# Moving VectorE's pieces, a split W2 load, SyncE stores and a cyclic field order in a three-layer CIN tower

## The reference

```python
def _cin_layer(X0, Xi, W, b):            # X0 (512, 39, 16), Xi (512, 39 or 128, 16)
    Wr = W.reshape(H, F0_, Fi)           # H = 128
    return jnp.einsum('hjk,bjd,bkd->bhd', Wr, X0, Xi) + b[None, :, None]

Xi = X0
for W, b in Ws:                          # three layers
    Xi = _cin_layer(X0, Xi, W, b)
    res.append(Xi.sum(axis=2))
z = jnp.concatenate(res, axis=1)         # (512, 384)
h = jnp.concatenate([z, dense_ctx], axis=1)
h = jnp.maximum(h @ W_top1 + b_top1, 0.0)
h = jnp.maximum(h @ W_top2 + b_top2, 0.0)
y = h @ W_top3
```

## Time and profile before

| | us |
|---|---|
| median of three runs | 679.05 |
| the profiled execution, whole | 682.02 |
| its span, first to last instruction | 680.2 |
| TensorE busy | 631.0 |
| VectorE busy | 582.5 |
| ScalarE busy | 549.5 |
| GpSimd busy | 431.7 |

### The profile page before, as it was taken

How to read it: one execution, slowest core, us unless ns; L and a number is a source line. 1 busy time by engine, 2 the same in 40 slices (tenths; PEclk the granted TensorE clock), 3 DMA queues, 4 the chain that set the end, 5 groups by cost and what they waited for, 6 DMA issues and landing times.

```text
span 680.2 us, 14168 instructions
## 1 busy us (share of the span) xinstructions
PE 631.0 (93%) x2563; PEld 473.1 (70%) x2563; DVE 582.5 (86%) x1229; ACT 549.5 (81%) x1735; POOL 431.7 (63%) x409
## 2 busy tenths in 40 slices
PE   0489799999999999999999999999999999999998
PEld 0157577777777777777777777777777777767583
DVE  0558769999989898999999999989898989999880
ACT  2057498989898989889898989898989889898682
POOL 6758396868868686868595968868685636220000
PEclk9989989999999999999999999999999999999999
DMA  6533712223140404040312223140404031000200
GB/s 219 140 78 81 229 47 74 68 51 89 27 115 9 131 3 124 16 119 21 94 47 63 78 53 88 25 116 8 132 2 128 9 106 32 12 17 0 63 0 1
DMA packets 42545, 46.14 MB, mean 68 GB/s; under 512 B 20705, under 2 KB 25409, under 8 KB 42378
## 3 DMA queue, kind: packets, MB, share of 16 engines
q1 hardware_dynamic: 26146, 42.28, 21.1%
q0 software_dynamic: 5120, 1.32, 2.4%
q10 hardware_dynamic: 11239, 2.05, 1.7%
HBM read 44.30 MB, written 1.31 MB: 67 GB/s over the span
## 4 chain that ended last, share of the span: by engine, by line
PE 54%; issue 20%; DVE 16%; DVEq 5%; DMA 2%; SPq 1%; POOL 1%; ACT 0%; ACTq 0%; POOLq 0%
DVE chain L614 8%; PE ya L493 7%; PE ya L494 6%; PE ya L495 6%; PE acc L469 6%; PE yd L493 5%; PE yd L495 5%; PE yd L494 5%; PE misc L476 3%; DVE z L641 2%; DVEq L146 2%; DVE prods L614 2%; DMA x0a<-x_rows 2%; DVEq L614 1%; DVE chain L612 1%
## 5 line engine op out<-in xcount | busy, mean ns | idle before, releaser
L740 ACT ACTIVATE prods<-ya,x0t 128x128 f32<-128x128 f32 x1472 | 451.6, 509 | 64.5 <-PE ya L495 59.9
L614 DVE SCALAR_TENSOR_TENSOR chain<-yd,x0t,chain 128x128 f32<-128x128 f32 x768 | 218.5, 344 | 16.3 <-PE yd L495 10.7
L301 POOL TENSOR_TENSOR prod<-tiles,x0a 120x512 f32<-120x512 f32 x105 | 136.6, 1302 | 83.5 <-DMA tiles<-x_rows 66.4
L493 PE MATMUL ya<-w1h,x1h 128*128 128x512 f32 (+1 forms) x384 | 173.8, 452 | 7.9 <-ACT prods L740 5.8
L373 POOL DMA_INDIRECT emb<-in_tables,rows x160 | 157.1, 982 | 36.3 <-issue 27.1
L494 PE MATMUL ya<-w1l,x1h 128*128 128x512 f32 (+1 forms) x384 | 147.9, 385 | 0.0
L495 PE MATMUL ya<-w1h,x1l 128*128 128x512 f32 (+1 forms) x384 | 147.5, 384 | 0.0
L629 DVE TENSOR_REDUCE x2t<-prods 128x128 f32<-128x1792 f32 x64 | 129.2, 2019 | 8.7 <-ACT prods L740 6.3
L493 PE MATMUL yd<-w1h,x1h 128*128 128x512 f32 x256 | 104.6, 409 | 11.1 <-DVE prods L614 6.7
L629 DVE TENSOR_REDUCE prods<-prods 128x128 f32<-128x1536 f32 x64 | 111.8, 1747 | 0.0
L408 POOL TENSOR_TENSOR prod0l<-prod,prod0h 120x512 fp32r<-120x512 f32 x70 | 91.1, 1301 | 27.1 <-ACT prod0h L749 26.9
(11 more groups left out here) (96 smaller groups left out, 602.8 us busy)
## 6 DMA issues: line engine op xcount, KB each, us to landing
tiles<-x_rows SPq DMA_DIRECT2D x236, 78.0 KB
x0a<-x_rows SPq DMA_DIRECT2D x45, 80.0 KB
emb<-in_tables,rows POOLq DMA_INDIRECT x160
w<-in_w SPq DMA_DIRECT2D x3, 832.0 KB
w<-in_w SPq DMA_DIRECT2D x1, 2496.0 KB, 12.8
tiles<-x_rows SPq DMA_DIRECT2D x32, 42.0 KB
x<-x_rows SPq DMA_DIRECT2D x16, 78.0 KB
x<-x_rows SPq DMA_DIRECT2D x16, 77.8 KB
```

Source lines behind the costliest of these rows:

```text
L301: engine.tensor_tensor(prod0[:, i % L0_PRODS, :], tiles[:, slot, :], x0a[:, :], ALU.mult).then_inc(prod0_ready, 1)
L493: pe.matmul(out, x1h[:, c % 2, xs], w1h[:, cols], start=True, stop=False)
L614: dve.scalar_tensor_tensor(out, product, x, run if step else b1[:, :], ALU.mult, ALU.add).then_inc(yd_used, 1)
L740: mm = act.activation(prods[:, :, slot_of(q) + i], ya[(NA * g + k) % YA][:, i * H:(i + 1) * H], ACT.Copy, scale=turned(c)[:, g * F1 + j:g ...
```

## The change

1. **VectorE's pieces.** `sum_dims` moves from group 1 to group 2, behind D block 3. `split_x1` moves from group 3 behind D block 6 to group 3 behind D block 3.
2. **W2 in 13 pieces** of three fields (192 KB), one after the loads of each chunk from 2 to 14.
3. **Stores on SyncE.** The store of a chunk's rows is issued by SyncE instead of ScalarE, as four DMAs instead of two: rows 40 to 59 of the scratch repeat rows 0 to 19.
4. **A cycle of 40.** Shifts are taken modulo 40 (39 fields and the padding row, whose weight is zero), as `tile + 7u`. With the repeated rows no shift wraps, so tile i and tile i+1 are the same rows one further, and one DMA of 40 partitions by 4 KB loads two of them. A chunk takes 12 tile DMAs instead of 28. In chunk 0 the last three tiles get places of their own in `gram`.
5. **The start.** Three matmuls (`WARM`) on TensorE after chunk 0's rows are stored; `turn_x0(0)` after layer-0 step 5 instead of 2; for chunk 0 ScalarE makes the rounded half straight from `acc0`, and VectorE makes the low half in two parts, so that TensorE's group 0 waits for the first 128 columns only; the low part of `w0` is made after that.

```diff
+SHIFTS = 7
+XR = FP + FP // 2
-TURN_0 = 2
+TURN_0 = 5
+WARM = 3
+W2_PARTS = 13
+BATCHES = ((0, 2), (2, 4), (4, 6), (6, 7))
+SUM_DIMS, SPLIT_X1 = (2, 0), (3, 0)
...
-def segments(i):
...
+        def load_tiles(engine, x, b):
+
+            first, end = BATCHES[b]
+            wait_done(engine, prod0_ready, max(uses_before(i, L0_TILES, x) for i in range(first, end)) if x else 0)
...
+            for u in range(3):
+                row = x * XR + SHIFTS * u + first
+                rows_on = bass.AP(scratch.tensor, row * COLS, [[COLS, R0], [1, (end - first) * COLS]])
+                engine.dma_start(to[u * R0:(u + 1) * R0, :, :].rearrange("p i n -> p (i n)"), rows_on).then_inc(tile_in[b], 16)
...
             def load_layer0(x, nxt):
 
-                sp.wait_ge(scratch_in, 2 * 16 * (x + 1))
+                sp.wait_ge(scratch_in, 4 * 16 * (x + 1))
                 wait_done(sp, prod0_ready, T0 * x)
                 load_x0a(sp, x)
-                for i in range(T0):
-                    load_tile(sp, x, i)
+                for b in range(len(BATCHES)):
+                    load_tiles(sp, x, b)
                 if nxt:
+                    store_x0(x + 1)
                     load_x0(x + 1)
...
             sp.wait_ge(w1_split, W1_PARTS)
-            sp.dma_start(w2[:, :, :], a["w2"]).then_inc(w2_in, 16)
             for x in range(2, CHUNKS):
                 load_layer0(x, x + 1 < CHUNKS)
+                if x - 2 < W2_PARTS:
+                    part = slice((x - 2) * F // W2_PARTS, (x - 1) * F // W2_PARTS)
+                    sp.dma_start(w2[:, part, :], a["w2"][:, part, :]).then_inc(w2_in, 16)
...
+            pe.wait_ge(w1_split, 1)
+            pe.wait_ge(scratch_in, 4 * 16)
+            for _ in range(WARM):
+                pe.matmul(ya[YA - 1][:, :], const[:, C_ID:C_ID + P], w1_raw[:, 0:COLS], start=True, stop=True)
...
                             multiply_add(c, g, q)
                             if q != own[0]:
+                                if (g, half) == SUM_DIMS:
+                                    sum_dims(c)
+                                if nxt and (g, half) == SPLIT_X1:
+                                    split_x1(c + 1)
                                 continue
-                            if nxt and (g, half) == (GROUPS - 1, 1):
-                                split_x1(c + 1)
...
+            for groups, done in ((slice(0, 1), x1_first), (slice(1, GROUPS), x1_split)):
+                cols = slice(groups.start * P, groups.stop * P)
+                dve.scalar_tensor_tensor(x1l[:, 0, cols].rearrange("p (g n) -> p g n", n=P), by_group[:, groups, :], bias[:, 0:1],
+                                         x1h[:, 0, cols].rearrange("p (g n) -> p g n", n=P).bitcast(F32),
+                                         ALU.add, ALU.subtract).then_inc(done, 1)
```

More of the change, by code:

```diff
@@ L93, in turn_after @@
     return (3, 1)
-def segments(i):
-    ends = [F - 3 * i + F * u for u in range(SEGMENTS - 1)]
-    return [((3 * i + a) % F, a, b) for a, b in zip([0] + ends, ends + [K0])]
 def fields_of(q):
@@ L245, in build @@
         gathered = [sem(f"gathered{i}") for i in range(2)]
-        tile_in = [sem(f"tile_in{i}") for i in range(L0_TILES)]
+        tile_in = [sem(f"tile_in{i}") for i in range(len(BATCHES))]
         bias2d_ready = sem("bias2d_ready")
@@ L296, in multiply0 @@
                 engine.wait_ge(x0a_in, 3 * 16 * (x + 1))
-            slot = i % L0_TILES
-            engine.wait_ge(tile_in[slot], 16 * SEGMENTS * (x * len(range(slot, T0, L0_TILES)) + i // L0_TILES + 1))
+            b = [i < end for _, end in BATCHES].index(True)
+            engine.wait_ge(tile_in[b], 3 * 16 * (x + 1))
             kind, count = products_free(x, i)
             wait_done(engine, prod0_split if kind == "split" else l0_done, count)
-            engine.tensor_tensor(prod0[:, i % L0_PRODS, :], tiles[:, slot, :], x0a[:, :],
+            engine.tensor_tensor(prod0[:, i % L0_PRODS, :], tile_of(x, i), x0a[:, :],
                                  ALU.mult).then_inc(prod0_ready, 1)
@@ L309, in _, with store_x0 @@
         def _(sp):
+            def store_x0(x):
+                sp.wait_ge(x0_ready, x + 1)
+                for first, count in ((0, FI), (FI, FI // 2)):
+                    by_row = chunk_rows(x)[first * FO:(first + count) * FO, :].rearrange("(f o) n -> f (o n)", f=count)
+                    for i, cols in enumerate((slice(0, FT * COLS), slice(FT * COLS, FO * COLS))):
+                        sp.dma_start(by_row[:, cols].rearrange("f (p b) -> p f b", b=CB),
+                                     xt[0:(cols.stop - cols.start) // CB, i, 0:count * CB].rearrange("p (f b) -> p f b", f=count),
+                                     ).then_inc(scratch_in, 16)
             def load_x0(x):
-                sp.wait_ge(scratch_in, 2 * 16 * (x + 1))
+                sp.wait_ge(scratch_in, 4 * 16 * (x + 1))
                 wait_done(sp, x0t_done, x)
@@ L500, in chunk @@
                 for g in range(GROUPS):
-                    if g == 0:
+                    if g == 0 and not prev:
+                        pe.wait_ge(x1_first, 1)
+                    if g == (0 if prev else 1):
                         pe.wait_ge(x1_split, c + 1)
@@ L661, in chunk @@
                                 sum_half(c - 1, GROUPS - 1, 1)
-                            if (g, half) == (1, 0):
-                                sum_dims(c)
             dve.wait_ge(w0_in, 16)
@@ L677, in _ @@
                               ALU.subtract).then_inc(w0_split, 1)
-            dve.wait_ge(bias_in, 3 * 16)
-            split_x1(0)
             chunk(0, False, True)
@@ L780, in _ @@
             evacuate_layout(0)
-            act.wait_ge(scratch_in, 2 * 16)
+            act.wait_ge(scratch_in, 4 * 16)
             load_x0a(act, 0)
-            for i in range(1, L0_TILES, 2):
-                load_tile(act, 0, i)
+            load_tiles(act, 0, 1)
+            load_tiles(act, 0, 3)
             evacuate_x0t(0)
@@ L831, in layer0_layout @@
     w = w.reshape(H, F, F)
-    pair = np.zeros((K0, 2, T0, H), np.float32)
-    i = np.arange(F)
+    pair = np.zeros((3, R0, 2, T0, H), np.float32)
     for tile in range(T0):
         for u in range(3):
-            shift = 3 * tile + u
-            if shift > F // 2:
-                continue
-            pair[R0 * u:R0 * u + F, 0, tile] = w[:, i, (i + shift) % F].T
-            if shift:
-                pair[R0 * u:R0 * u + F, 1, tile] = w[:, (i + shift) % F, i].T
+            shift = tile + SHIFTS * u
+            for i in range(F):
+                j = (i + shift) % R0
+                if j == F or (2 * shift == R0 and i > j):
+                    continue
+                pair[u, i, 0, tile] = w[:, i, j]
+                if shift:
+                    pair[u, i, 1, tile] = w[:, j, i]
     return pair.reshape(K0, 2, T0 * H)
```

55 lines of the change are left out of this document (30 added, 25 removed).

## The result

The changed kernel takes 672.94 us (median of four runs, 671.37 to 673.52) against 679.04 before; the ratio is 0.990, with a 95% interval of 0.987 to 0.993. It is 6.1 us faster where 24.9 were forecast, and lies outside the forecast range of 646 to 662. The profiled execution took 673.33 us, with a span of 671.5 (before 680.2), so the spans differ by 8.7 us. That is 2.6 more than the medians do: the profiled execution of before stood 3.0 us above its median, this one 0.4. TensorE was busy for 630.4 us, VectorE 580.1, ScalarE 544.1, GpSimd 432.5.

The account below looks back on a forecast made before the run. The prediction took TensorE as the bound, with stalls on VectorE, one long W2 wait and a slow start; -7.6 - 12.0 - 4.8 - 0.8 + 0.3 = -24.9 us from 679.05 gave 654.1 us, range 646 to 662.

Parts of the forecast that it names:

- All three signs of being wrong: Forecast wrong if the chunk stays above 36 us, `turn_x0` waits, or layer 1 starts after 39.
- What bounds the kernel: TensorE, busy 631.0 of 680.2 us; two VectorE stalls cost 1.22 us a chunk, which without stalls needs 35.18.
- W2 in pieces: -7.6: TensorE's 5.76 us gap at chunk 2's first product, behind the W2 load, goes: -7.6 us, range -8 to -5.6.
- VectorE's pieces: -12.0: Moving `sum_dims` and `split_x1` cuts TensorE's stalls by 0.85 us a chunk: -12.0 us, range -7 to -17.
- all stalls go: Rival: VectorE is never behind, so TensorE's steady-chunk stalls all vanish; 648 us, chance 0.11.
- Loads in a cycle of 40: 0: Steady-chunk tile loads: first product 0.4 us late, covered by ScalarE's lead; 0, range 0 to +4 for all chunks.
- The start: -4.8: Before layer 1: layer 0 ends 3.7 us earlier and the way to layer 1 shortens by 1.1; range -2 to -6.
- The hand-over's -1.1: Between layer 0 and layer 1 in chunk 0: 2.35 us shrinks to 1.2 in all, -1.1 us.
- The clock behind the start: -0.8: After TensorE's pause before layer 1: half of an estimated 1.6 us half-clock loss saved; range 0 to -1.6.
- cover in chunk 0: +0.3: Chunk 1's products come at most 4.9 us earlier, TensorE 5.6; slack covers the difference: +0.3, range 0 to +2.
- Stores on SyncE: 0: Two more stores take 0.8 to 1 of some 1.4 us spare before TensorE's turn of `x0`; 0, range 0 to +5.
- The rival on the slow side: Each chunk waits for the store: `x0` late for TensorE's turn in group 3; 690 us, chance 0.03.

Follow-up runs that it names:

- e3_w2_early: The changed kernel with each W2 piece issued behind the tile loads, ahead of SyncE's wait for the store: 663.26 us, ratio 0.978.
- e5_rows32_8: The changed kernel with each tile DMA of 40 rows cut into one of 32 and one of 8: 667.71 us, ratio 0.981.
- e7_no_warm: The changed kernel without the three `WARM` matmuls ahead of layer 0: 671.53 us, ratio 0.986.
- e13_evac_again: Second run of the kernel before plus VectorE's pieces, W2 in 13 pieces and chunk 0's new rounded and low halves, old loads and stores: 653.68 us, ratio 0.964.
- e4_first_alone: The changed kernel with the first pair of tiles loaded as two single tiles, pairs only after them: 657.09 us, ratio 0.969.

## Why the prediction was wrong, point by point

All three signs of being wrong that it named came: the chunk stayed above 36 us (36.22), `turn_x0` waited (once), and layer 1 started after 39 (44.12). Two steps failed, the loads' cover and the start.

**What bounds the kernel.** Right. TensorE without stalls needs 35.25 us a chunk (I read 35.18), and both VectorE stalls had the causes named: moving the two pieces alone takes them away.

**W2 in pieces: -7.6.** Right in the main: the gap has gone, and the chunk with it lost 8.1 us. Of this W2 in pieces makes 6.2 by the experiments (42.24 to 36.07) and VectorE's pieces 2.7; the changed kernel's own chunk is 0.7 above that (36.77), since its product is late here too.

**VectorE's pieces: -12.0.** The mechanism was right and the size too small: alone they give 1.15 a chunk, not 0.85. The term of 8.34 us a group was a distance between two rows of the timeline and held idle time: VectorE was busy for 8.07 us of it (the row at 170.33 shows 0.19 idle). With 8.07 the prediction's sum is 4 x 8.07 + 1.04 + 0.66 = 34.0 us instead of 35.06, and the kernel with the pieces moved shows 34.07. So VectorE had a microsecond to catch up with. The rival "all stalls go" was the true case here. In the changed kernel this gain was nearly all lost again.

**Loads in a cycle of 40: 0.** This is the step that failed first: a delay of the first product that was costed at nothing. "The product ends at about 157, 0.4 us late, and ScalarE's own lead over the banks' need covers that." The 157 stood against an end at 155.02 (153.72 + 1.30) before, 2.0 us later, with 1.6 to spare at ScalarE, and the three prices named ahead of it (1, 0.8 and 1) even add to 2.8. Measured from the transpose of `lay_out` the product of the chunk shown starts 3.8 us later (14.69 against 10.93 us; by the medians 3.3, 14.68 against 11.40), of which the stores make 0.3. The pair with the W2 piece ahead of it costs more than the two prices added. And ScalarE's lead covers 1.26 us of its wait, no more. That can be read chunk by chunk: in the four kernels e3_w2_early, e5_rows32_8, e7_no_warm and the changed one ScalarE waited for 1.3 us or more in 36 steady chunks, and wait less excess of the chunk over 35.25 us has a median of 1.26, half of them within 1.23 to 1.28; in the chunk above it is 1.97 - 0.70. The ten chunks with a shorter wait are as short as without one, but for one. With 2.06 us of waiting on average the changed kernel's chunk is 36.22 us against the 35.27 of the kernel with items 1 and 2. That is 0.95 us a chunk and 11.4 over the twelve (434.68 against 423.25 us). The range, 0 to +4 for all chunks, gave this term no room to be a wait of every chunk, though the working itself had the spare time used up.

**The start: -4.8.** Wrong by 7.7 us, and the second step that failed: TensorE was to run seven steps from 28.1 without a wait, but waited 3.71 us for the second pair. The first product came at 28.40 instead of 27.5. The second pair, part of what was to be in by 31.6, was used at 34.09. The stretch from 24 to 34 moved 2.15 MB at 215 GB/s: the sum had 1.92 MB at 234 and left out `x0`'s 0.23. That the second pair came only with the last of it fits loads that share the engines, but no trace shows when a single load landed, so this stays a reading. What `WARM` gave, two steps in half the time, was lost in the wait behind it. Single first tiles give 3.7 us of it back (40.45). The 1.3 us for issue and wake-up stand in no row; the smallest loads of the trace before took 1.7 us from issue to landing. The hand-over's -1.1 was right: 1.07 by both pairs of kernels.

**The clock behind the start: -0.8, and cover in chunk 0: +0.3.** The clock stayed at full speed over 42 to 46 (0.50 over 44 to 46 before), so all of the estimated 1.6 us was gained. But the cover failed by as much: this stretch takes 20.22 us, where e13_evac_again, with its clock kept too, takes 57.02 - 38.40 = 18.62, and e4_first_alone 18.93. Chunk 1's first product came at 54.27 instead of 49.06, and TensorE waited for it:

```profile
55.68 1.10 PE L494 MATMUL acc<-prod,w 120*128 120x512 f32 x2 [1.34 <-POOL prod L313]
```

**Stores on SyncE: 0.** Right in what it asked of `x0`. Store to `x0` issue takes 2.98 us instead of 2.54, and TensorE's turn waited once, for 0.38 us.

**The rival on the slow side** had the right shape, a link of loads that every chunk waits for, but it was set at `x0` and TensorE's turn, and its chance at 0.03. The link was the next one in the same chain: from `x0` over the W2 piece and `x0a` to the first pair, GpSimd and ScalarE.

## What to carry to other kernels

Packing more into the first DMA of a batch delays the first thing that anyone needs; load the first tiles singly, and pack those behind them. Fewer DMAs gain nothing by themselves where the engine that issues them isn't waited for: 15 a chunk instead of 28 brought no time here. Before a transfer is costed at nothing, subtract its delay from the spare time of the instruction that waits for it, on an engine that works in order, and where the rest is below zero, count it in every chunk. A distance between two rows of a busy engine's timeline is no work time as long as idle time stands in brackets between them.
